# Scores of head pairs on partition halves, low half of the attended rows on GpSimd, and a reordered start, in a gated cross-attention and feed-forward kernel

## The chip, the cores and the metric

The kernel runs on one core of a Trainium2 chip. The time is device microseconds of one execution; the profile comes from one profiled execution. TensorE is called PE below, VectorE DVE, ScalarE ACT, GpSimd POOL and SyncE SP. SP mostly issues DMAs.

## What is computed

```
# x, ctx: 16 batches of 256 rows x 256 columns, fp32
x = x + tanh(g_xattn) * attention(layernorm(x), ctx, ctx)   # 16 heads of 16 dims, softmax
x = x + tanh(g_ffn) * ffn(layernorm(x))                     # 4-bit weights, 16-bit activations

attention:  q = Q @ Wq.T + bq; k = K @ Wk.T + bk; v = V @ Wv.T + bv
            scores = q @ k.T / sqrt(16); attn = softmax(scores)
            out = (attn @ v) @ Wo.T + bo
ffn:        gate, up, product and sums are rounded to 16 bits by a scale over the whole tensor
```

## The kernel before, in words

`attention` computes the first line for all 16 batches and leaves y and its LayerNorm (`lnall`); `feed_forward` computes the second. The change touches `attention` only, and the order in which the host lays out the columns of Wq, Wk and their biases.

Precision: each fp32 operand of a projection is split into a high and a low fp16 part, and three products are summed (high x high, high x low, low x high), so one projection is 12 matmuls of 256 columns (`project`, `split_product`, L418). ACT makes the high part of a result out of PSUM (`high`, `high_of`), DVE (or POOL) the low part (`low`, `low_of`).

The order of work is written out by hand as one software pipeline. All engines walk the same list of steps, `STEPS = range(-40, PAIRS * NB + 31)`. A step g is one pair of heads of one batch; a batch has 8 steps. `batch(g, off)` gives the batch whose work with offset `off` falls on step g. In steady state the work of a step depends on g mod 8 only; "step 0" to "step 7" below mean this number. On PE, each step has these parts in this order:

- the scores of batch it+1 for the maximum (L516): q and k of the pair are stacked on partitions as high, high, low of q against high, low, high of k, 96 rows. Four matmuls of 256 columns: two query tiles (tt) x two heads of the pair (r). Both heads of one tile go to one PSUM bank, `s_ps[tt]`. The two heads share the rows of `kst`; `qst` holds two copies, in which the rows of the other head are zero (the third index, r). DVE reduces each bank to the row maxima (`negm`, L880) and increments `max_done`; a bank may be written again when its own reduction is done.
- the transposed scores of batch it (L531), two matmuls of 512 columns (both heads), 97 rows: the 97th holds ones in `kst` and the negated maximum in `qst`. ACT takes the exponential (L694) into `pt`.
- in steps 5, 7, 1 and 3 the projections of v, of the output, of q and of k (the last three for other batches; L418)
- in steps 2, 4, 6 and 0 the values (L455): 16 matmuls of fp32 that write 32 partitions each
- in steps 4 and 0 the transposes of the maxima (L431), in step 6 the transposes of the normalised x (L591, `xn`).

DVE does the two reductions of the step first and then: y (step 0), its statistics (1), the low half of q (2), statistics of x (3), the low half of k and the reciprocal of the denominators (4), the low half of the attended rows `al` (5, `low_of`, L838), the maximum over `lnall` (6), the low half of x (7); in steps 5 to 7 of the first nine batches also work on the feed-forward weights. POOL does in steps of its own: `cl` (1, L1019), `at` (2), the root and LayerNorm of y (2, L988, L990, L1038), `normalise` for x (step 4, L988, L990, L999), which waits for the transposes of step 6 (`xt_done`), `xb` (6), weight pieces (7 and 0). The LayerNorm is `(x - mean) * rstd` in one instruction.

SP issues per batch: the stack of q in 6 DMAs (`stack_q`, 2 heads x 3), the stack of k in 3 (`stack_k`), the maxima in 2 x 2 (`load_tops`), and loads and stores. PE waits at step 0 for `stack_loaded`. Before step 0 of batch 0 lies a start in which weights are split, an identity matrix is built through DRAM (`ident_dram`), batch 0 is projected (q, then k, then v), and stacks are set to zero.

Of the kernel before, what the change touches and what calls it, by code (L numbers as in the profile page):

```python
# [5 lines left out]
ALU = mybir.AluOpType  # L6
# [10 lines left out]
P = 128  # L17
# [12 lines left out]
def attention(nc, t, x, ctx, out):  # L30
# [26 lines left out]
    with ExitStack() as es:  # L57
# [30 lines left out]
        ones = sb("ones", [P, 1], F32)  # L88
# [7 lines left out]
        rstd = sb("rstd", [P, KT], F32)  # L96
        xh = sb("xh", [P, 2, S], F16)
# [5 lines left out]
        kst = sb("kst", [97, 3, PAIRS, S], F16)  # L103
        qst = sb("qst", [97, 3, 2, PAIRS, S], F16)
# [18 lines left out]
        rstd2 = sb("rstd2", [P, 2, KT], F32)  # L123
        recl = sb("recl", [P, 2, 16], F32)
# [29 lines left out]
        zeros_written = sem("zeros_written")  # L154
        ones_written = sem("ones_written")
# [3 lines left out]
        qst_zeroed = [sem(f"qst_zeroed{i}") for i in range(3)]  # L159
        half_set = sem("half_set")  # L160
        w_loaded = sem("w_loaded")
# [83 lines left out]
        rstd2_done = sem("rstd2_done")  # L245
        ln_done = sem("ln_done")
        lnmax_done = sem("lnmax_done")
        lmax_done = sem("lmax_done")
        lmax_turned = sem("lmax_turned")
        ltop_done = sem("ltop_done")  # L250
        ltop_spread = sem("ltop_spread")
# [27 lines left out]
        ident_dram = nc.dram_tensor("ident_dram", (P * P,), F32, kind="Internal").ap()  # L279

# [3 lines left out]
        def _(sp):  # L284
# [11 lines left out]
            def stack_q(b):  # L296
                n = b % 3
                sp.wait_ge(qh_done, b + 1)
                if b >= 3:
                    sp.wait_ge(st_done, UNITS * (b - 2))  # L300
                sp.wait_ge(qst_zeroed[n], 1)
                for d, i in enumerate((0, 0, 1)):
                    if d == 2:
                        sp.wait_ge(ql_done, b + 1)
# [37 lines left out]

            load_x(0)
            sp.wait_ge(ident_zeroed, 2)
            sp.dma_start(ident_dram.rearrange("(p q) -> p q", p=P), ident[:]).then_inc(zeros_written, 16)
            for n in "qkv":
                sp.dma_start(wf[n], t["w" + n].rearrange("(t p) e -> p t e", p=P)).then_inc(w_loaded, 16)
            load_c(0)
            sp.wait_ge(zeros_written, 16)
            sp.dma_start(ident_dram[0:P * P:P + 1].rearrange("(p o) -> p o", o=1), ones[:],  # L350
                         allow_slow_non_contiguous=True).then_inc(ones_written, 16)
            load_x(1)
            sp.dma_start(bqk[:, 0, :], t["bq"]).then_inc(b_loaded, 16)
            sp.dma_start(bqk[:, 1, :], t["bk"]).then_inc(b_loaded, 16)
            sp.wait_ge(ones_written, 16)
            sp.dma_start(ident[:], ident_dram.rearrange("(p q) -> p q", p=P)).then_inc(ident_set, 16)
            load_c(1)
            sp.dma_start(wstage[:].rearrange("p (f d) -> p f d", d=D),
                         t["w_gate"].rearrange("(f p) d -> p f d", p=P)).then_inc(wn_loaded[0], 16)
# [4 lines left out]
            sp.dma_start(bvc[:], t["bv"]).then_inc(wo_loaded, 16)  # L364

# [48 lines left out]
        def _(pe):  # L414
# [89 lines left out]
            pe.wait_ge(ident_set, 16)  # L504
            for g in STEPS:
                it, j = divmod(g, PAIRS)
                if 0 <= it + 1 < NB:
                    b = it + 1
                    if j == 0:
                        pe.wait_ge(stack_loaded[b % 2], 144 * (b // 2 + 1))  # L510
                    for tt in range(KT):
                        u = UNITS * b + KT * j + tt
                        if u >= 2:
                            pe.wait_ge(max_done, u - 1)
                        for r in range(2):
                            mm = nc.tensor.matmul(s_ps[tt][:, r, :], qst[0:96, b % 3, r, j, tt * P:(tt + 1) * P],  # L516
                                                  kst[0:96, b % 3, j, :], start=True, stop=True)
                        mm.then_inc(s_done, 1)
                if 0 <= it < NB:
                    b = it  # L520
                    if g == 0:
                        pe.wait_ge(ones_set, 1)
                    if j == 0:
                        pe.wait_ge(top_loaded[0], 32 * (b + 1))
                    if j == QA:
                        pe.wait_ge(top_loaded[1], 32 * (b + 1))
                    for kt in range(KT):
                        u = UNITS * b + KT * j + kt
                        if u >= 3:
                            pe.wait_ge(exp_done, u - 2)  # L530
                        nc.tensor.matmul(st_ps[u % 3][:], kst[:, b % 3, j, kt * P:(kt + 1) * P],  # L531
                                         qst[:, b % 3, :, j, :], start=True, stop=True).then_inc(st_done, 1)

                if (b := batch(g, V)) is not None:
# [3 lines left out]
                    pe.wait_ge(weights_low, 3)  # L538
# [11 lines left out]
                if (b := batch(g, Q)) is not None:  # L550
                    pe.wait_ge(y_done, before(g, PROJ))
                    pe.wait_ge(v_taken, before(g, V))
                    pe.wait_ge(ql_done, b)
# [1263 lines left out]
```

## Time and profile before

| | us |
|---|---|
| median of 3 runs (600.8, 605.62, 606.33) | 605.62 |
| the profiled execution, its time | 602.64 |
| the profiled execution, its span | 600.80 |
| busy: PE / DVE / ACT / POOL | 561.2 / 490.0 / 438.6 / 206.3 |
| attention stage, first to last instruction (chain of waits enters the feed-forward) | 0 to 331.2 |
| feed-forward stage | 331.2 to 600.8 |

An instruction's time in the profile is from its start to its end; matmuls are pipelined, so that several of them overlap, and the distance of their starts says what each costs the engine. "x4" in a timeline row means that four instructions are merged, and the time is that of all of them. Idle time of an engine before an instruction stands in brackets with what ended it.

### The profile page before, as it was taken

What the parts mean: (1) busy time and instruction counts of PE and PEld (TensorE: products, weight loads), DVE (VectorE), ACT (ScalarE), POOL (GpSimd) and SP (SyncE); (2) the same over time, 40 slices, a digit from 0 to 9 for tenths busy, and PEclk for the clock granted to TensorE, in tenths of its full rate; (3) what the DMA queues carried; (4) which work ended last, traced back from release to release, by engine and by line L of the source; (5) the groups of instructions that cost most, each with busy time, mean ns of one, the idle gap of its engine ahead of it and who ended that gap; (6) DMA issues with size and microseconds to landing.
All of it is one profiled execution on the core that took longest, in us unless ns stands there. A gap on an engine that the chain in (4) does not pass through costs nothing. (4 is left out here: it accounts for less than half of the span.)

```text
span 600.8 us, 11772 instructions
## 1 busy us (share of the span) xinstructions
PE 561.2 (93%) x4337; PEld 341.6 (57%) x4337; DVE 490.0 (82%) x832; ACT 438.6 (73%) x633; POOL 206.3 (34%) x227
## 2 busy tenths in 40 slices
PE   1679999999999999999987999999999899989998
PEld 1446666666666666666446444444444344458887
DVE  5688889999999988999838699979987799964542
ACT  2227888788788877888675344549999998889960
POOL 3722358766667879765346000000000000010100
PEclk9989999999999999999999899999999999999999
DMA  6532444454554454333231000000000000023443
GB/s 184 148 89 83 134 130 128 127 145 129 152 147 140 132 139 126 96 105 109 71 102 71 3 0 1 0 1 1 1 1 0 1 0 1 0 71 106 141 141 106
DMA packets 42812, 48.98 MB, mean 82 GB/s; under 512 B 10436, under 2 KB 30532, under 8 KB 42756
## 3 DMA queue, kind: packets, MB, share of 16 engines
q1 hardware_dynamic: 40916, 43.38, 24.6%
q0 software_dynamic: 1408, 4.46, 2.6%
q8 instruction: 35, 0.57, 0.4%
q10 hardware_dynamic: 432, 0.39, 0.3%
q14 instruction: 21, 0.17, 0.1%
HBM read 24.32 MB, written 8.70 MB: 55 GB/s over the span
## 5 line engine op out<-in xcount | busy, mean ns | idle before, releaser
L880 DVE TENSOR_REDUCE negm<-s_ps 128x2 bf16<-128x512 f32 x256 | 163.1, 681 | 21.3 <-PE s_ps L516 20.1
L694 ACT ACTIVATE pt<-st_ps 128x512 f32<-128x512 f32 x256 | 138.8, 596 | 48.0 <-PE st_ps L531 46.8
L1218 PE MATMUL pairs<-xq,wut 128*128 128x512 f16 x576 | 124.7, 379 | 2.7 <-ACT lnall L1412 1.6
L1218 PEld LDWEIGHTS pairs<-xq,wut 128*128 128x128 f16 x576 | 56.2, 98 | 71.1 <-issue 2.3
L516 PE MATMUL s_ps<-kst,qst 96*128 96x256 f16 x512 | 80.7, 275 | 8.9 <-DVE negm L880 5.5
L531 PE MATMUL st_ps<-qst,kst 97*128 97x512 f16 x256 | 76.5, 380 | 1.3 <-ACT pt L694 0.8
L455 PE MATMUL pv_ps<-pt,vt 128*32 128x256 f32 x1024 | 68.5, 385 | 1.4 <-ACT ot L638 0.7
L1732 POOL PARTITION_ALL_REDUCE vmax<-vmax x5 | 1.8, 355 | 193.1 <-DVE vmax L1525 119.4
L516 PEld LDWEIGHTS s_ps<-kst,qst 96*128 96x128 f16 x512 | 44.4, 98 | 31.7 <-DVE negm L880 18.3
L1218 PE MATMUL pairs<-xq,wgt 128*128 128x512 f16 x276 | 60.5, 379 | 0.0
L999 POOL TENSOR_SCALAR xn<-xt,mv,rstd 128x256 f32<-128x256 f32 x30 | 36.5, 1223 | 55.5 <-PE misc L591 55.3
L1324 PE MATMUL pairs<-wdt,h 128*128 128x256 f16 x384 | 47.2, 273 | 2.9 <-DVE h L1687 2.3
L455 PEld LDWEIGHTS pv_ps<-pt,vt 128*32 128x32 f32 x1024 | 26.9, 109 | 38.8 <-issue 25.3
L1352 ACT COPY gb<-pairs 128x1024 f32<-128x1024 f32 x24 | 24.3, 1012 | 32.6 <-PE pairs L1218 32.6
L1218 PEld LDWEIGHTS pairs<-xq,wgt 128*128 128x128 f16 x276 | 26.8, 98 | 31.1
L1324 PEld LDWEIGHTS pairs<-wdt,h 128*128 128x128 f16 x384 | 37.3, 98 | 8.1 <-issue 2.8
L631 ACT ACTIVATE qk<-misc,bqk_s 128x256 f16<-128x256 f32 x64 | 26.9, 473 | 15.7 <-PE misc L418 15.7
L1038 POOL TENSOR_SCALAR lnall<-y,mv,rstd 128x256 f32<-128x256 f32 x28 | 34.4, 1235 | 1.5
L1594 DVE CUSTOM_DVE_ANT_0 gb<-lnall 128x1024 f32<-128x1024 int16 x24 | 29.1, 1219 | 7.0 <-ACT lnall L1384 6.8
L1587 DVE TENSOR_REDUCE cmax<-pairs 128x1 f32<-128x1024 f32 x24 | 29.3, 1222 | 1.6 <-PE pairs L1218 1.6
L1412 ACT ACTIVATE lnall<-pairs,scal 128x1024 int16<-128x1024 f32 x23 | 25.3, 1110 | 5.9 <-PE pairs L1218 5.8
L785 DVE SCALAR_TENSOR_TENSOR qk<-misc,bqk_s,qk 128x256 f16<-128x256 f32 x64 | 27.8, 476 | 2.2 <-ACT qk L631 2.2
(217 smaller groups left out, 1032.9 us busy)
## 6 DMA issues: line engine op xcount, KB each, us to landing
qst<-qk SPq DMA_DIRECT2D x96, 64.0 KB, 2.0
kst<-qk SPq DMA_DIRECT2D x45, 128.0 KB, 3.2
xt<-in_x SPq DMA_DIRECT2D x16, 256.0 KB, 4.3
ct<-in_ctx SPq DMA_DIRECT2D x16, 256.0 KB, 2.9
xr<-in_x SPq DMA_DIRECT2D x16, 256.0 KB, 4.1
out<-y SPq DMA_DIRECT2D x16, 256.0 KB, 4.0
lnall<-out POOLq DMA_DIRECT2D x8, 512.0 KB, 4.2
recb<-rec_dram SPq DMA_DIRECT2D x15, 256.0 KB
```

The source lines that it names most:

```text
L455: mm = nc.tensor.matmul(pv_ps[32 * c:32 * c + 32, u % 2, :], vt[:, b % 3, kt, 8 * (c // 2) + 2 * u + c % 2, :], pt[:, u % 2, c // 2, kt, c ...
L516: mm = nc.tensor.matmul(s_ps[tt][:, r, :], qst[0:96, b % 3, r, j, tt * P:(tt + 1) * P], kst[0:96, b % 3, j, :], start=True, stop=True)
L531: nc.tensor.matmul(st_ps[u % 3][:], kst[:, b % 3, j, kt * P:(kt + 1) * P], qst[:, b % 3, :, j, :], start=True, stop=True).then_inc(st_done, 1)
L694: nc.scalar.activation(pt[:, (j // 2) % 2, j % 2, kt], st_ps[u % 3][:], ACT.Exp, scale=1.0 / (WS * WS * HD ** 0.5)).then_inc(exp_done, 1)
L785: op = nc.vector.scalar_tensor_tensor(out=qk[:, 2 * i + 1, e, :], in0=frm[:, e, :], scalar=bqk_s[:, i, e:e + 1], in1=qk[:, 2 * i, e, :], o ...
L880: nc.vector.tensor_reduce(negm[:, b % 2, tt, lo:lo + 5:4], s_ps[tt][:], AX.X, ALU.max, negate=True).then_inc(max_done, 1)
L999: op = nc.gpsimd.tensor_scalar(xn[:, tt, :], xt[:, b % 3, tt, :], mv[:, tt, 0:1], rstd[:, tt:tt + 1], ALU.subtract, ALU.mult)
L1038: nc.gpsimd.tensor_scalar(t["lnall"][:, b, tt * D:(tt + 1) * D], y[:, b % 2, tt, :], mv2[:, b % 2, tt, 0:1], rstd2[:, b % 2, tt:tt + 1], A ...
L1218: mm = nc.tensor.matmul(ps[:, p, k, :], w[:, a, dt, f * P:(f + 1) * P], xq[:, b, c, dt, :], start=n == 0, stop=n == len(terms) - 1)
L1324: mm = nc.tensor.matmul(to, lh, wdt[:, h, f, :], start=n == 0, stop=n == len(terms) - 1)
L1587: nc.vector.tensor_reduce(cmax[:, 1, PR * c + p:PR * c + p + 1], ps[:, p], AX.XY, ALU.max, apply_absolute_value=True).then_inc(u_max, 1)
L1594: nc.vector.tensor_tensor_reduce(gb[:, c, 2 * p:2 * p + 2].rearrange("p f w -> p (f w)"), ia[:, d, 2 * p:2 * p + 2].rearrange("p f w -> p ...
```

## The change

1. Scores: `kst` and `qst` become 128 rows high. The high, high and low rows of a head dimension lie on neighbouring partitions (4k, 4k+1, 4k+2), the first head of a pair on partitions 0 to 63, the second on 64 to 127; row 63 and row 127 hold ones and the maximum. There is one copy of q. A score matmul has 63 rows, a transposed one 64; all have 256 columns, and the heads alternate. A PSUM bank of the scores now holds one head for both query tiles.
2. The stacks are 3 DMAs each for q and k, the maxima 1 instead of 2.
3. `al` moves from DVE to POOL (same step, 5, ahead of `xb`).
4. LayerNorm on POOL becomes `x * rstd + shift`, with `shift = -mean * rstd` computed by two instructions on 128x2. `normalise` moves from step 4 to step 7.
5. The start: each weight has its own semaphore; the identity is made by POOL (`affine_select`); k of batch 0 is projected ahead of q, into `st_ps[0]`; `cl` of batch 0 is made on DVE; kst and qst are zeroed whole; 12, 4 and 5 spare matmuls of 512 columns are put on PE; ACT issues the first stacks; gate work moves from steps -12 and -10 to -6 and -5.

The diff, cut to its core:

```diff
-        kst = sb("kst", [97, 3, PAIRS, S], F16)
-        qst = sb("qst", [97, 3, 2, PAIRS, S], F16)
+        kst = sb("kst", [P, 3, PAIRS, S], F16)
+        qst = sb("qst", [P, 3, PAIRS, S], F16)
...
             def stack_q(b):
                 for d, i in enumerate((0, 0, 1)):
...
-                    for r in range(2):
-                        lo = 32 * d + r
-                        sp.dma_start(qst[lo:lo + 31:2, n, r].rearrange("p j q -> p (j q)"),
-                                     qk[r:P:2, i].rearrange("p h q -> p (h q)")).then_inc(stack_loaded[b % 2], 16)
+                    sp.dma_start(qst[d:P:4, n].rearrange("p j q -> p (j q)"),
+                                 qk[:, i].rearrange("p h q -> p (h q)")).then_inc(stack_loaded[b % 2], 16)
             def stack_k(b):
...
-                    sp.dma_start(kst[32 * d:32 * d + 32, n].rearrange("p j q -> p (j q)"),
+                    sp.dma_start(kst[d:P:4, n].rearrange("p j q -> p (j q)"),
             def load_tops(b, hf):
-                for r in range(2):
-                    sp.dma_start(qst[96:97, b % 3, r, QA * hf:QA * hf + QA, :], mrow[QA * r:QA * r + QA, hf, :]
-                                 ).then_inc(top_loaded[hf], 16)
+                sp.dma_start(qst[63:P:64, b % 3, QA * hf:QA * hf + QA, :], mrow[:, hf, :]).then_inc(top_loaded[hf], 16)
...
+            def spare_products(n):
+                for _ in range(n):
+                    nc.tensor.matmul(s_ps[0][:].rearrange("p a b -> p (a b)"), kst[0:63, 1, 0, 0:P],
+                                     kst[0:63, 1, 0:2].rearrange("p j q -> p (j q)"), start=True, stop=True)
+            pe.wait_ge(kst_zeroed, 1)
+            spare_products(12)
+            pe.wait_ge(weights_low, 1)
+            pe.wait_ge(cl_done, 1)
+            project(st_ps[0], "k", ch, cl, k_done)
+            spare_products(4)
+            pe.wait_ge(ident_set, 1)
...
                     for tt in range(KT):
-                        u = UNITS * b + KT * j + tt
-                        if u >= 2:
-                            pe.wait_ge(max_done, u - 1)
                         for r in range(2):
-                            mm = nc.tensor.matmul(s_ps[tt][:, r, :], qst[0:96, b % 3, r, j, tt * P:(tt + 1) * P],
-                                                  kst[0:96, b % 3, j, :], start=True, stop=True)
-                        mm.then_inc(s_done, 1)
+                            u = UNITS * b + 2 * j + r
+                            if tt == 0 and u >= 2:
+                                pe.wait_ge(max_done, u - 1)
+                            mm = nc.tensor.matmul(s_ps[r][:, tt, :], qst[64 * r:64 * r + 63, b % 3, j, tt * P:(tt + 1) * P],
+                                                  kst[64 * r:64 * r + 63, b % 3, j, :], start=True, stop=True)
+                            if tt == KT - 1:
+                                mm.then_inc(s_done, 1)
...
                     for kt in range(KT):
-                        u = UNITS * b + KT * j + kt
-                        if u >= 3:
-                            pe.wait_ge(exp_done, u - 2)
-                        nc.tensor.matmul(st_ps[u % 3][:], kst[:, b % 3, j, kt * P:(kt + 1) * P],
-                                         qst[:, b % 3, :, j, :], start=True, stop=True).then_inc(st_done, 1)
+                        for r in range(2):
+                            u = UNITS * b + 2 * j + r
+                            if kt == 0 and u >= 3:
+                                pe.wait_ge(exp_done, u - 2)
+                            mm = nc.tensor.matmul(st_ps[u % 3][:, kt, :],
+                                                  kst[64 * r:64 * r + 64, b % 3, j, kt * P:(kt + 1) * P],
+                                                  qst[64 * r:64 * r + 64, b % 3, j, :], start=True, stop=True)
+                            if kt == KT - 1:
+                                mm.then_inc(st_done, 1)
...
+                    if b == 0:
+                        spare_products(5)
+                        pe.wait_ge(weights_low, 2)
                     pe.wait_ge(xl_done, b + 1)
                     project(bank(g), "q", xh, xl, q_done)
-                if (b := batch(g, K)) is not None:
+                if (b := batch(g, K)) is not None and b:
...
-                if (b := batch(g, 21)) is not None and b < LAST - 1:
-                    low_of(b)
...
+                nc.gpsimd.tensor_scalar(negative, r, -1.0, 0.0, ALU.mult, ALU.add).then_inc(done, 1)
+                pool.wait_ge(done, 2 * b + 1)
+                nc.gpsimd.tensor_tensor(to, mean, negative, ALU.mult).then_inc(done, 1)
+                pool.wait_ge(done, 2 * b + 2)
...
-                        op = nc.gpsimd.tensor_scalar(xn[:, tt, :], xt[:, b % 3, tt, :], mv[:, tt, 0:1],
-                                                     rstd[:, tt:tt + 1], ALU.subtract, ALU.mult)
+                        op = nc.gpsimd.tensor_scalar(xn[:, tt, :], xt[:, b % 3, tt, :], rstd[:, tt:tt + 1],
+                                                     shift[:, tt:tt + 1], ALU.mult, ALU.add)
...
+            nc.gpsimd.affine_select(out=ident[:], in_=ident[:], compare_op=ALU.not_equal, fill=1.0, base=0,
+                                    pattern=[[-1, P]], channel_multiplier=1).then_inc(ident_set, 1)
...
+            nc.gpsimd.memset(qst[:].rearrange("p n j q -> p (n j q)").bitcast(I32), 0).then_inc(qst_zeroed, 1)
...
+                if (b := batch(g, 21)) is not None and b < LAST - 1:
+                    pool.wait_ge(ah_done, b + 1)
+                    pool.wait_ge(o_done, b)
+                    nc.gpsimd.tensor_tensor(al[:], at[:, b % 2], ah[:], ALU.subtract).then_inc(al_done, 1)
...
-                if (b := batch(g, -28)) is not None and b:
+                if (b := batch(g, -25)) is not None and b >= 2 or g == PAIRS - 28 and (b := 1):
                     normalise(b)
```

## Rows read from the trace of the kernel before

**Rows 1.** Table of windows: length, busy time and instructions of each engine, clock, DMA.
```profile
core 0: us, PE busy (x) PEld busy (x) DVE busy (x) ACT busy (x) POOL busy (x), PEclk, DMA share, GB/s
43.00:285.69 242.69, 239.93 (x2309) 157.28 (x2309) 222.93 (x459) 196.62 (x406) 157.01 (x167) 1.00 0.44 125
111.02:128.33 17.31, 17.31 (x170) 11.52 (x168) 16.23 (x36) 13.64 (x28) 12.49 (x14) 1.00 0.46 134
```

**Rows 2.** Timeline of PE, one batch: start, length, engine, line, operation, count.
```profile
111.02 0.60 PE L516 MATMUL s_ps<-kst,qst 96*128 96x256 f16 x4
...
113.08 0.61 PE L516 MATMUL s_ps<-kst,qst 96*128 96x256 f16 x4
...
115.28 0.60 PE L516 MATMUL s_ps<-kst,qst 96*128 96x256 f16 x4
...
117.24 0.61 PE L516 MATMUL s_ps<-kst,qst 96*128 96x256 f16 x4
...
123.69 0.60 PE L516 MATMUL s_ps<-kst,qst 96*128 96x256 f16 x4
...
126.15 0.60 PE L516 MATMUL s_ps<-kst,qst 96*128 96x256 f16 x4
```

**Rows 3.** Timeline of PE from one step's transposed scores to the next step's.
```profile
102.56 0.60 PE L531 MATMUL st_ps<-qst,kst 97*128 97x512 f16 x2
103.09 1.07 PE L455 MATMUL pv_ps<-pt,vt 128*32 128x256 f32 x16
103.98 0.27 PE L431 MATMUL misc<-identb,negm 128*8 128x128 bf16 x2
104.19 0.61 PE L516 MATMUL s_ps<-kst,qst 96*128 96x256 f16 x4
104.63 0.60 PE L531 MATMUL st_ps<-qst,kst 97*128 97x512 f16 x2
105.07 0.38 PE L418 MATMUL misc<-wh_v,ch 128*128 128x256 f16 x2
```

**Rows 4.** Timeline of DVE, reductions of the same batch.
```profile
113.62 1.28 DVE L880 TENSOR_REDUCE negm<-s_ps 128x2 bf16<-128x512 f32 x2
...
115.76 1.26 DVE L880 TENSOR_REDUCE negm<-s_ps 128x2 bf16<-128x512 f32 x2
...
117.72 1.28 DVE L880 TENSOR_REDUCE negm<-s_ps 128x2 bf16<-128x512 f32 x2
...
119.92 1.26 DVE L880 TENSOR_REDUCE negm<-s_ps 128x2 bf16<-128x512 f32 x2
...
122.14 1.22 DVE L880 TENSOR_REDUCE negm<-s_ps 128x2 bf16<-128x512 f32 x2
...
124.23 1.23 DVE L880 TENSOR_REDUCE negm<-s_ps 128x2 bf16<-128x512 f32 x2
...
126.57 1.29 DVE L880 TENSOR_REDUCE negm<-s_ps 128x2 bf16<-128x512 f32 x2 [0.42 <-PE s_ps L516]
```

**Rows 5.** Groups of instructions by line: count, busy us, mean ns, idle before.
```profile
L1038 POOL TENSOR_SCALAR lnall<-y,mv,rstd 128x256 f32<-128x256 f32 x28 | 34.4, 1235 | 1.5
...
L990 POOL TENSOR_TENSOR rstd<-ve,half 128x2 f32<-128x2 f32 x32 | 22.9, 717 | 2.7
...
L1019 POOL TENSOR_TENSOR cl<-ct,ch 128x512 f16<-128x512 f32 x15 | 17.3, 1154 | 8.5 <-ACT ch L720 8.5
...
L838 DVE TENSOR_TENSOR al<-at,ah 128x512 f16<-128x512 f32 x15 | 12.0, 802 | 3.7 <-ACT ah L661 3.7
...
L988 POOL TENSOR_SCALAR ve<-mv 128x2 f32<-128x2 f32 x32 | 6.2, 195 | 32.3 <-DVE mv L758 21.1 <-issue 7.6 <-DVE mv L806 1.4
```

**Rows 6.** Timeline of all engines, the start up to the first scores.
```profile
10.59 1.11 PE L591 MATMUL misc<-ident,xn 128*128 128x128 f32 x4 [10.59 <-DMA ident<-ident_dram]
...
17.01 0.88 DVE L785 SCALAR_TENSOR_TENSOR qk<-misc,bqk_s,qk 128x256 f16<-128x256 f32 x2 [2.21 <-ACT qk L631]
...
19.97 1.99 ACTq L707 DMA_DIRECT2D kst<-qk  x3
...
25.78 0.61 PE L516 MATMUL s_ps<-kst,qst 96*128 96x256 f16 x4 [2.58 <-DMA kst<-qk]
```

More of the change, by code:

```diff
@@ L158, in attention @@
         ones_set = sem("ones_set")
-        qst_zeroed = [sem(f"qst_zeroed{i}") for i in range(3)]
+        kst_zeroed = sem("kst_zeroed")
+        qst_zeroed = sem("qst_zeroed")
         half_set = sem("half_set")
-        w_loaded = sem("w_loaded")
+        wk_loaded = sem("wk_loaded")
+        wq_loaded = sem("wq_loaded")
+        wv_loaded = sem("wv_loaded")
         b_loaded = sem("b_loaded")
@@ L341, in spread_rec, with load_w @@
                              ).then_inc(rec_loaded, 16)
+            def load_w(n, done):
+                sp.dma_start(wf[n], t["w" + n].rearrange("(t p) e -> p t e", p=P)).then_inc(done, 16)
             load_x(0)
[L344 to L352, printed above, removed]
+            load_w("k", wk_loaded)
             sp.dma_start(bqk[:, 0, :], t["bq"]).then_inc(b_loaded, 16)
             sp.dma_start(bqk[:, 1, :], t["bk"]).then_inc(b_loaded, 16)
[L355 to L359, printed above, removed]
+            load_c(0)
+            load_w("q", wq_loaded)
+            load_w("v", wv_loaded)
+            load_x(1)
             sp.dma_start(gx[:], t["gx"].rearrange("(o d) -> o d", o=1).broadcast_to((P, 1))).then_inc(g_loaded, 16)
@@ L676, in _ @@
                     if b:
-                        act.wait_ge(stack_loaded[(b - 1) % 2], 144 * ((b - 1) // 2 + 1))
-                    act.wait_ge(bias_scaled, 1)
+                        act.wait_ge(stack_loaded[(b - 1) % 2], 96 * ((b - 1) // 2 + 1))
                     high(0, bank(PAIRS * b + Q), qh_done)
-                if (b := batch(g, -12)) is not None:
+                    if b == 0:
+                        act.wait_ge(qst_zeroed, 1)
+                        act.wait_ge(ql_done, 1)
+                        act.dma_start(qst[2:P:4, 0].rearrange("p j q -> p (j q)"),
+                                      qk[:, 1].rearrange("p h q -> p (h q)")).then_inc(stack_loaded[0], 16)
+                if (b := batch(g, -12)) is not None and b:
                     act.wait_ge(k_done, b + 1)
@@ L690, in _ @@
                         act.wait_ge(pv_done, 4 * b + j // 2 - 1)
-                    for kt in range(KT):
-                        u = UNITS * b + KT * j + kt
+                    for r in range(2):
+                        u = UNITS * b + 2 * j + r
                         act.wait_ge(st_done, u + 1)
-                        nc.scalar.activation(pt[:, (j // 2) % 2, j % 2, kt], st_ps[u % 3][:], ACT.Exp,
+                        nc.scalar.activation(pt[:, (j // 2) % 2, j % 2, :, r], st_ps[u % 3][:], ACT.Exp,
                                              scale=1.0 / (WS * WS * HD ** 0.5)).then_inc(exp_done, 1)
@@ L857, in _, with weight_low @@
             nc.vector.memset(ident[:], 0.0).then_inc(ident_zeroed, 1)
-            nc.vector.memset(ones[:], 1.0).then_inc(ident_zeroed, 1)
             nc.vector.memset(half[:], -0.5).then_inc(half_set, 1)
             nc.vector.memset(row1[:], 1.0).then_inc(half_set, 1)
+            nc.vector.memset(kst[:].rearrange("p n j q -> p (n j q)").bitcast(I32), 0).then_inc(kst_zeroed, 1)
+            nc.vector.memset(ones16[:].bitcast(I32), ONES).then_inc(kst_zeroed, 1)
             normal_stats(0)
-            nc.vector.memset(qst[:, 1].rearrange("p r j q -> p (r j q)").bitcast(I32), 0).then_inc(qst_zeroed[1], 1)
+            def weight_low(n, m):
+                dve.wait_ge(weights_high, m)
+                nc.vector.scalar_tensor_tensor(out=wl[n][:], in0=wf[n][:], scalar=WS, in1=wh[n][:],
+                                               op0=ALU.mult, op1=ALU.subtract).then_inc(weights_low, 1)
+            weight_low("k", 1)
+            dve.wait_ge(ch_done, 1)
+            nc.vector.tensor_tensor(cl[:], ct[:, 0], ch[:], ALU.subtract).then_inc(cl_done, 1)
+            dve.wait_ge(b_loaded, 32)
+            nc.vector.tensor_scalar(bqk_s[:], bqk[:], WS, None, ALU.mult).then_inc(bias_scaled, 1)
+            weight_low("q", 2)
             dve.wait_ge(rstd_done, 1)
@@ L867, in _ @@
             op.then_inc(xn_ready, 1)
-            for n, m in zip("qkv", range(3)):
-                dve.wait_ge(weights_high, m + 1)
-                nc.vector.scalar_tensor_tensor(out=wl[n][:], in0=wf[n][:], scalar=WS, in1=wh[n][:],
-                                               op0=ALU.mult, op1=ALU.subtract).then_inc(weights_low, 1)
+            dve.wait_ge(kh_done, 1)
+            dve.wait_ge(bias_scaled, 1)
+            low(1, st_ps[0], kl_done)
             for g in STEPS:
@@ L891, in _ @@
                     normal_stats(b)
-                if (b := batch(g, -12)) is not None:
+                if (b := batch(g, -12)) is not None and b:
                     dve.wait_ge(kh_done, b + 1)
```

116 lines of the change are left out of this document (64 added, 52 removed).

## The prediction

> **What bounds the kernel now.** I read the table of windows first, then the timeline of one batch on TensorE and on VectorE. The program has two stages. The feed-forward from 331 us on is not touched by the diff. The attention stage is. In its steady part, the 14 batches from 43.00 to 285.69 us, PE is busy 239.93 of 242.69 us, DVE 222.93, ACT 196.62 and POOL 157.01; one batch of eight steps takes 17.31 us, with PE busy for all of it and DVE for 16.23 [rows 1]. The starts of the score matmuls say that it is an issue limit and not a chain of waits: step 0 takes 113.08 - 111.02 = 2.06 us, step 1 2.20, step 2 1.96, step 6 126.15 - 123.69 = 2.46 [rows 2]. Steps 3, 5 and 7 are like step 1 and step 4 is like step 0, which adds up: 2 x 2.06 + 4 x 2.19 + 1.96 + 2.46 = 17.3. So PE is the bound, and DVE is only 1.08 us per batch behind it. What is saved on PE pays until DVE takes over.
>
> **The scores on PE.** Per step, the four 256-column score matmuls (96 rows) take 104.63 - 104.19 = 0.44 us, and the two 512-column ones for the exponentials (97 rows) take 105.07 - 104.63 = 0.44 [rows 3]: 0.11 us for 256 columns in both. After the change the two heads of a pair lie on partitions 0-62 (63) and 64-126 (127), in turn, into different banks. If the two halves of the array work side by side, each group needs two rounds of 0.11 instead of four: 0.22 + 0.22 saved, 0.44 us per step. The trace of before has no matmul on row halves. Bounds: nothing saved (they run in turn, as all matmuls on the full array do here), or 0.44. The nearest row for the good end is the value product: its 16 matmuls, on four column groups, take only 103.98 - 103.09 = 0.89 us [rows 3], a quarter of 16 single 0.22 us slots (3.5). I take 0.44, since these run side by side already.
> The Trainium skill ("TensorE: Matmul & The Clock Gate", part 3 on packing small matmuls) says the same of row groups; no run so far shows it for them.
>
> **What the halves cost.** Two 512-column matmuls from 102.56 would be through at 102.56 + 0.44 = 103.00; the value products begin at 103.09. After them two 128-column matmuls from 103.98 are through at 104.09, and the scores begin at 104.19 [rows 3]. So going into and out of the column groups costs 0.1 us each. Now the scores are a shape of their own too. Steps 1, 3, 5 and 7 (scores, then a full-array projection) get two more changes of shape, step 6 one more (its transposes on the full array stand ahead of the next scores), steps 0, 2 and 4 none, because their neighbours are value products or the 8-column turns of the maxima, which follow the value products without a gap. Nine changes at 0.1 us are 0.9 us per batch. Bounds: 0, and 0.25 each (2.2).
> The Trainium skill ("TensorEngine Tiling (Array Packing)", key properties under tiling modes) has the rule that speaks against the change: a change of tiling mode drains TensorE. The page gives no price. Two 256-column matmuls take 0.38 us of which 0.22 is their turn on the array [rows 3], so a full emptying would be 0.16 us: 1.4 us per batch instead of 0.9. The rows show 0.1, and the sum goes by them; what the rule says happens is what they show.
> New step times of PE alone: steps 0 and 4 2.06 - 0.44 = 1.62; step 2 1.52; odd steps 2.20 - 0.44 + 0.2 = 1.96; step 6 2.46 - 0.44 + 0.1 = 2.12. Sum 14.7 us per batch.
>
> **DVE takes over.** Where DVE had no wait, the distance from one pair of reductions to the next is DVE's own step: 115.76 - 113.62 = 2.14 in step 1, 1.96 in step 2, 2.20 in step 3, 2.22 in step 4, 2.09 in step 5, 126.57 - 124.23 - 0.42 idle = 1.92 in step 6 [rows 4]. The change takes the low half (0.80 us in the mean of 15 [rows 5]) out of step 5.
> There is also a new lock step. Now each bank holds one head for both query tiles, and the matmuls alternate between the banks, so the first pair already needs both reductions of the step before; until now the first bank was refilled under the second reduction. From the scores' start to the reduction is 126.57 - 126.15 = 0.42 us [rows 2, 4]; the pair of reductions takes 1.28; for the semaphore I take 0.08, as the gap of 0.09 above. So no step is shorter than 0.42 + 1.28 + 0.08 = 1.78 us. A step's other DVE work (y, statistics, low halves of q and k, transposed x) lies in that gap and hides it where it is 0.6 us or more. Only step 5, emptied of its low half, shows it, and there PE's 1.96 is longer.
> Taking the longer of the two engines in each step: 1.8, 2.14, 1.96, 2.20, 2.22, 1.96, 2.12, 1.96 = 16.4 us. I add 0.1 for the steps in which the preparation of the feed-forward weights lies (DVE work of steps 5 and 6 in the first nine batches): 16.5. Fourteen batches: 242.7 - 231.0 = 11.7 us saved. Bounds per batch: DVE's bare 16.23 - 0.80 = 15.4, and 17.5 if the other DVE work comes too late to fill half of the gaps.
>
> **POOL.** It gets the low half; the same operation for the context takes 1.15 us on POOL [rows 5]. The LayerNorm as multiply-add needs two more operations on 128x2 each time, twice a batch: four, between 0.20 (the small scalar operation) and 0.72 each (the power), so 0.8 to 2.9 us; I take 1.1, as a plain multiply is nearer to the first. The large operation itself was 1.23 us; as multiply and add it lies between 0.6 (half of the 512 elements of the 1.15 us row) and 1.25; I take 1.2, for the sum does not hang on it. POOL then has 12.49 + 1.15 + 1.1 = 14.7 us in a batch of 16.5. Its waits for the transposes (normalise sits one stage ahead of them now, and is moved from step 4 to step 7, behind them) go. What hangs on it, `al` before the output projection of step 7, and `lnall` before the maximum of step 6, is then about a step early. So nothing is charged. If that cover is gone (upper end, 16.5 us of work), PE waits for `al`: some 0.5 us per batch.
> SP issues three q stacks instead of six and one row of maxima instead of two, so the queue that also carries the k stack is emptier. The steps being shorter takes 0.7 us from the k stack's way between its low half and its first use, and the three issues saved give that back. I charge nothing.
>
> **The start.** Now the identity goes through DRAM, transposes start at 10.59, the low half of q is done at 17.01 + 0.88, k's comes after it and its stack is issued at 19.97; scores start at 25.78, 5.81 later [rows 6]. After: POOL makes the identity, the transposes also need its reciprocal root, so I leave them near 10.6. K's projection is ahead of x's, on a PE kept busy by spare products. Left is q's path: low half at 17.9, or 16 if the projection runs at full speed (four transposes of 1.11 us show that PE is slow there [rows 6]); then one DMA on ACT's queue instead of three, about 3.6 us to the first score. That is 19.6 to 21.5; I take 19.7, since the spare products are many: 6.1 us saved. Bounds: 3 (the zeroing of all of qst on POOL, and the second x, become the last), and 8. The batch behind it, 43.00 - 25.78 = 17.2, I put at 16.7: 0.5 saved. The tail after 285.69 has no score reductions for most of its length and hangs on ACT and DMA: 0.5 saved.
>
> **Sum.** 6.1 + 0.5 + 11.7 + 0.5 = 18.8 us. The profiled execution took 602.64 us (span 600.80 and 1.84 around it): 583.8. The median shown is 605.62, 3 us above it, with runs from 600.8 on: against it 586.8. I forecast 585.5, between them.
>
> **Rivals.**
> 1. The halves don't overlap (the change doesn't do what it says). Then PE keeps its 17.31 and gets the nine changes of shape: 18.2 us per batch, 14 x 0.9 = 12.6 slower, about 1 more in the two ends, less 6.1 at the start: 602.6 + 7.5 = 610. It decides if the second matmul of a pair starts about 0.11 us behind the first; break-even is 17.7 us a batch. For it: nothing on row halves in the trace; against: the column groups overlap. Chance 0.08.
> 2. The lock step costs in most steps: 17.3 to 17.5 us per batch, and only the start gains: 602.6 - 6.6 + 1 = 597. For it: DVE within 8% of PE before, and DVE work that itself waits for ACT in the same step (the low halves). Against: before, that work came without a wait. Chance 0.17.
> 3. DVE is never left waiting, 15.6 us a batch, POOL's traffic on it lower: 14 x 0.9 less, 573. For: DVE had slack only of its own making; against: PE is longer in steps 5 to 7. Chance 0.10.
> The forecast, 576 to 593, has 0.65.
>
> **Chances and range.** A measurement of this kernel tells about 1% from no change. Faster by over 1% means under 599.6: the forecast, rival 3 and most of rival 2 (0.12 of its 0.17): 0.87. Within 1%: 0.05, the upper end of rival 2. Slower: 0.08, rival 1. The range leaves out rival 1 and the ends of the others: 575 to 600.
>
> **What would show it.** Right: pairs of score matmuls within some 10 ns of each other; a batch of 16.2 to 16.8 us; DVE busy over 94% of it, with idle left before the reductions of steps 5 to 7; gaps of 0.1 us at the projections; first score near 20 us; `al` on POOL near 1.15. Wrong: pairs 0.11 us apart (rival 1); waits of the reductions for the scores in steps 1 to 4 (rival 2); PE waiting for `al` or for the k stack; first score after 23 us.

## The result and the profile after

The changed kernel takes 589.0 us (588.25 to 589.84, 4 runs), the one before 604.47 beside it (600.8 to 606.33, 4 runs): a ratio of 0.9745, interval 0.9714 to 0.9777. The profiled execution went from 602.64 to 588.25 us, 14.4 less.

The windows of the changed kernel, cut at the first score (21.47), the end of the first pass (40.90), the end of the steady part (271.89) and the start of the feed-forward (near 316.8); inside them the first batch of the steady part and one later batch. Columns: length, busy us (instructions) of PE, PE weight loads, DVE, ACT, POOL, then the granted clock as a share of full, DMA share, GB/s.

```profile
0.00:21.47 21.47, 14.71 (x66) 7.11 (x67) 12.30 (x32) 7.75 (x15) 9.16 (x18) 1.00 0.67 208
21.47:40.90 19.43, 14.30 (x79) 7.33 (x79) 15.10 (x31) 3.86 (x9) 5.40 (x12) 0.73 0.29 91
40.90:58.60 17.70, 16.33 (x157) 9.07 (x157) 14.08 (x30) 12.12 (x26) 3.45 (x7) 0.82 0.24 80
40.90:271.89 230.99, 219.71 (x2533) 133.26 (x2534) 218.44 (x447) 193.19 (x406) 148.38 (x224) 0.99 0.43 132
107.47:123.66 16.19, 15.63 (x185) 9.60 (x185) 15.68 (x35) 13.42 (x28) 12.13 (x19) 1.00 0.49 142
```

Beside [rows 1]: the 14 steady batches went from 242.69 to 230.99 us, 11.7 less, just what was forecast. The start gave 25.78 - 21.47 = 4.3 (forecast 6.1), the first pass took 19.43 instead of 17.22 (2.2 lost, 0.5 gained was forecast), the tail to the feed-forward gave 0.6 (forecast 0.5). That is 14.4 for a forecast of 18.8. Both misses lie before 40.90. The exact hit on the steady part has luck in it: its first batch took 17.70 us at a granted clock of 0.82 (15.80 at full clock, in `warm` below), a loss that the forecast didn't have, and the later ones made up for it.

One batch on PE, the rows that answer to [rows 2, 3]: start, us from first start to last end, then the operation.

```profile
107.47 0.39 PE L529 MATMUL s_ps<-kst,qst 63*128 63x256 f16 x4
...
109.11 0.53 PE L529 MATMUL s_ps<-kst,qst 63*128 63x256 f16 x4
...
111.00 0.38 PE L419 MATMUL misc<-xh,wl_q 128*128 128x256 f16 x2
111.32 0.39 PE L529 MATMUL s_ps<-kst,qst 63*128 63x256 f16 x4
111.54 0.38 PE L546 MATMUL st_ps<-qst,kst 64*128 64x256 f16 x4
111.86 1.07 PE L456 MATMUL pv_ps<-pt,vt 128*32 128x256 f32 x16
112.86 0.74 PE L529 MATMUL s_ps<-kst,qst 63*128 63x256 f16 x4
...
115.17 0.41 PE L529 MATMUL s_ps<-kst,qst 63*128 63x256 f16 x4
...
116.83 0.28 PE L529 MATMUL s_ps<-kst,qst 63*128 63x256 f16 x1
117.38 0.39 PE L529 MATMUL s_ps<-kst,qst 63*128 63x256 f16 x3 [0.27 <-DVE negm L924]
...
118.15 0.39 PE L419 MATMUL misc<-wh_v,ch 128*128 128x256 f16 x2 [0.17 <-DVE qk L818]
...
119.57 0.39 PE L529 MATMUL s_ps<-kst,qst 63*128 63x256 f16 x4
```

Four score matmuls of 256 columns now have their turn in 111.54 - 111.32 = 0.22 us, where four took 0.44 before: the halves of the array work side by side. After the last pair (0.22 from 111.00) the next shape would start at 111.22 and starts at 111.32; after the scores at 111.76 the value products start at 111.86. A change of shape is 0.10 us here too.

The same stretch on DVE, which answers to [rows 4]:

```profile
107.90 1.29 DVE L924 TENSOR_REDUCE negm<-s_ps 128x2 bf16<-128x512 f32 x2
...
109.76 1.28 DVE L924 TENSOR_REDUCE negm<-s_ps 128x2 bf16<-128x512 f32 x2
...
111.90 1.26 DVE L924 TENSOR_REDUCE negm<-s_ps 128x2 bf16<-128x512 f32 x2
...
113.85 1.28 DVE L924 TENSOR_REDUCE negm<-s_ps 128x2 bf16<-128x512 f32 x2
...
116.06 1.26 DVE L924 TENSOR_REDUCE negm<-s_ps 128x2 bf16<-128x512 f32 x2
117.23 0.87 DVE L818 SCALAR_TENSOR_TENSOR qk<-misc,bqk_s,qk 128x256 f16<-128x256 f32 x2
...
118.27 1.23 DVE L924 TENSOR_REDUCE negm<-s_ps 128x2 bf16<-128x512 f32 x2
...
120.00 1.30 DVE L924 TENSOR_REDUCE negm<-s_ps 128x2 bf16<-128x512 f32 x2
...
122.13 1.30 DVE L924 TENSOR_REDUCE negm<-s_ps 128x2 bf16<-128x512 f32 x2 [0.15 <-PE s_ps L529]
```

DVE has hardly a gap: 15.68 of 16.19 us, against PE's 15.63 (before: PE 17.31 of 17.31). Neither is full; they wait for each other for some 0.5 us each.

POOL's lines, with the mean ns of one, which answer to [rows 5]; each of the two new small operations on 128x2 takes 0.19 us:

```profile
L1081 POOL TENSOR_TENSOR al<-at,ah 128x512 f16<-128x512 f32 x14 | 16.2, 1157 | 29.7 <-ACT ah L682 29.7
L1089 POOL TENSOR_SCALAR lnall<-y,rstd,shift 128x256 f32<-128x256 f32 x28 | 15.3, 555 | 1.5
```

The start on PE, against [rows 6], and after it the row of q's low half on DVE:

```profile
4.39 5.30 PE L508 MATMUL s_ps<-kst 63*128 63x512 f16 x12 [4.39 <-DVE kst L893]
9.62 0.61 PE L419 MATMUL st_ps<-ch,wh_k 128*128 128x256 f16 x2
...
13.70 0.66 PE L612 MATMUL misc<-ident,xn 128*128 128x128 f32 x4
...
15.84 0.38 PE L419 MATMUL misc<-xh,wh_q 128*128 128x256 f16 x2 [0.31 <-DVE xl L975]
...
21.47 0.39 PE L529 MATMUL s_ps<-kst,qst 63*128 63x256 f16 x4 [0.44 <-DMA qst<-qk]
...
33.58 0.32 PE L529 MATMUL s_ps<-kst,qst 63*128 63x256 f16 x1 [2.38 <-DVE negm L924]
```

```profile
18.22 0.88 DVE L818 SCALAR_TENSOR_TENSOR qk<-misc,bqk_s,qk 128x256 f16<-128x256 f32 x2 [0.45 <-ACT qk L652]
```

The transposes stand at 13.70 instead of 10.59: twelve spare products hold PE until 9.69, k's projection runs at half speed (0.43 us per two from 9.62 on; the 1.00 in the table's first window doesn't show it, the starts do), four spares follow it, and only then come the transposes. From 13.70 on the way to the end of q's low half takes 5.4 us (18.22 + 0.88 = 19.10), as forecast (10.6 to 16), with q's projection at full speed (0.22 per two).

### The profile page after: what moved, and what is told of

It reads as the page before. It is cut to its first block and busy times, and to the rows that moved or that the text cites. A ratio compares the mean times of both kernels' runs of the same rounds, so it can differ in the third digit from the quotient of the medians.

```text
span 586.4 us, 12288 instructions
## 1 busy us (share of the span) xinstructions
PE 544.4 (93%) x4614; PEld 317.1 (54%) x4614; DVE 483.0 (82%) x818; ACT 435.1 (74%) x633; POOL 191.8 (33%) x298
## 5 line engine op out<-in xcount | busy, mean ns | idle before, releaser
L529 PE MATMUL s_ps<-kst,qst 63*128 63x256 f16 x512 | 66.9, 282 | 16.6 <-DVE negm L924 13.7
L546 PE MATMUL st_ps<-qst,kst 64*128 64x256 f16 x512 | 56.4, 272 | 1.7 <-ACT pt L732 1.7
L529 PEld LDWEIGHTS s_ps<-kst,qst 63*128 63x128 f16 x512 | 20.6, 94 | 54.7 <-DVE negm L924 39.7
L546 PEld LDWEIGHTS st_ps<-qst,kst 64*128 64x128 f16 x512 | 30.7, 96 | 6.8 <-ACT pt L732 3.7
L1688 DVE TENSOR_TENSOR gb<-lnall 128x1024 f32<-128x1024 int16 x23 | 27.2, 1216 | 2.5 <-ACT lnall L1468 2.4
L1700 DVE TENSOR_REDUCE cmax<-gb 128x1 f32<-128x2048 f32 (+2 forms) x16 | 27.8, 1746 | 0.0
```

The source lines that it names most:

```text
L529: mm = nc.tensor.matmul(s_ps[r][:, tt, :], qst[64 * r:64 * r + 63, b % 3, j, tt * P:(tt + 1) * P], kst[64 * r:64 * r + 63, b % 3, j, :], s ...
L546: mm = nc.tensor.matmul(st_ps[u % 3][:, kt, :], kst[64 * r:64 * r + 64, b % 3, j, kt * P:(kt + 1) * P], qst[64 * r:64 * r + 64, b % 3, j, ...
L1688: nc.vector.tensor_tensor(gb[:, c, 2 * p:2 * p + 2], ia[:, c % 2, 2 * p:2 * p + 2], ib[:, c % 2, 2 * p:2 * p + 2], ALU.mult).then_inc(p3_d ...
L1700: nc.vector.tensor_reduce(cmax[:, 3, n:n + 1], flat[:, first:last], AX.X, ALU.max, apply_absolute_value=True).then_inc(p3_max, 1)
```

## The experiments

Twelve kernels, in four groups; each group had its own runs of the kernel before beside it (medians 604.21, 603.53, 604.73 and 604.55 us). Ratios are to those, with 95% intervals. The first four went together, then `after_control` to `warm`, then `before_al_norm` to `warm_stats5`, then the last.

**same_half: both heads of a pair on one half.** Edit, the same at all four places of the scores (the second head's scores are then made from the first head's rows):

```diff
-qst[64 * r:64 * r + 63, b % 3, j, tt * P:(tt + 1) * P]
+qst[0:63, b % 3, j, tt * P:(tt + 1) * P]
```

> The changed kernel, but both heads of a pair use partitions 0 to 63 for the scores (the second head is computed from the first head's rows, so that half of the attention is of the wrong head; the number and sizes of the matmuls stay). If the gain comes from the two halves working side by side, the four score matmuls of a step take 0.44 us again instead of 0.22, both kinds, the batch goes from 16.2 to about 18.2 us (14.7 + 8 x 0.44 on TensorE), and the time to about 589 + 14 x 2 + 2 = 619 us, slower than the kernel before. If the gain came from the low half on GpSimd or from the start, the time stays within 3 us of 589.

619.87 us (2 runs), ratio 1.0246 (1.0177 to 1.0315). Window of one batch, and its first matmuls:

```profile
119.76:138.02 18.26, 18.26 (x186) 12.19 (x185) 16.00 (x35) 13.88 (x28) 11.77 (x19) 1.00 0.40 125
```

```profile
119.76 0.61 PE L529 MATMUL s_ps<-kst,qst 63*128 63x256 f16 x4
120.20 0.60 PE L546 MATMUL st_ps<-qst,kst 64*128 64x256 f16 x4
```

0.44 us for four again, PE busy for all of 18.26 us: 17.31 and the nine changes of shape. This is rival 1 made on purpose; its batch of 18.2 was right. With all the rest of the change in place, the one edit is worth 2.07 us a batch and 31 us in all.

**al_dve: the low half of the attended rows back on DVE, in step 5.**

```diff
-                    nc.gpsimd.tensor_tensor(al[:], at[:, b % 2], ah[:], ALU.subtract).then_inc(al_done, 1)
...
+                if (b := batch(g, 21)) is not None and b < LAST - 1:
+                    low_of(b)
```

> The changed kernel with the low half of the attended rows back on VectorE, in step 5. Theory: in step 5 TensorE is the longer one (its v projection waits for the low half of k), so the 0.7 us fit into VectorE's slack: 0 to 0.3 us per batch, 589 to 592 us. Rival: VectorE sets the batch and every us on it counts: 0.7 per batch, 599 us.

587.21 us, ratio 0.9718 (0.9679 to 0.9758); the changed kernel has 0.9745 (0.9714 to 0.9777).

```profile
107.12:123.31 16.19, 15.63 (x186) 9.60 (x186) 16.05 (x36) 13.43 (x28) 10.45 (x18) 1.00 0.44 140
```

The same 16.19 us, with DVE at 16.05 instead of 15.68. The move to POOL brings nothing: from step 5's reductions to step 6's DVE now takes 2.10 us instead of 1.73, and from there to step 7's 1.82 instead of 2.13. PE sets the pace there, and DVE has room.

**ln_old: the LayerNorms as before (subtract, then multiply), without the two small operations.**

```diff
-                                                     shift[:, tt:tt + 1], ALU.mult, ALU.add)
+                                                     rstd[:, tt:tt + 1], ALU.subtract, ALU.mult)
```

> The changed kernel with the LayerNorm on GpSimd in its old form (subtract, multiply; no shift). GpSimd gets 4 x 0.67 us more and 4 x 0.2 us less per batch, 1.9 us, 14.0 of 16.2 busy. Theory: its results are due a step later or more, so 588 to 591 us. Rival: GpSimd is on the path through the low half and the output projection, 1 us per batch or more, 603 us and up.

587.46 us, ratio 0.9721 (0.9678 to 0.9763), the batch 16.19 us. POOL has slack either way; nothing hangs on the form.

**r_outer: the score matmuls for the maxima ordered by head, then by tile**, so the first bank is filled before the second is needed.

```diff
-                    for tt in range(KT):
-                        for r in range(2):
+                    for r in range(2):
+                        for tt in range(KT):
```

> The changed kernel with the score matmuls for the maximum ordered by head first, tile second: a bank is filled again as soon as its own reduction is done, but two neighbours are on the same half. Theory: TensorE loses 0.1 us per step where it is the longer one, and gains 0.3 us where it waits for the second reduction now (steps 1, 3 to 5): 586 to 591 us. Rival (the lock step of both reductions is what keeps the batch at 16.2): 0.6 us per batch gained, 581 us.

586.77 us, ratio 0.9706 (0.9668 to 0.9744), the batch 16.19 us.

```profile
110.49 0.40 PE L529 MATMUL s_ps<-kst,qst 63*128 63x256 f16 x4
110.72 0.39 PE L546 MATMUL st_ps<-qst,kst 64*128 64x256 f16 x4
```

The four still pass in 0.23 us. I read it so that the second tile of the first head runs beside the first tile of the second head; that reading is argued, the 0.23 is measured. That starts need not keep the program's order shows elsewhere in this batch: a transposed score matmul starts at 108.51, the last of the four before it at 108.54. What follows is that the order of the four decides nothing here, and that a lock step between the banks costs nothing that this edit could give back.

**after_control: the changed kernel again**, beside those that follow.

> The changed kernel once more, on the same chip as the three beside it: 587 to 589 us, and again a long stretch at the lower clock after the first scores if that belongs to the kernel and not to the one execution.

589.43 us (587.59 to 592.53), ratio 0.9767 (0.9742 to 0.9793).

**before_al_pool: the kernel before, with only the low half moved to POOL.**

```diff
-                    low_of(b)
...
+                    nc.gpsimd.tensor_tensor(al[:], at[:, b % 2], ah[:], ALU.subtract).then_inc(al_done, 1)
```

> The kernel before with only the low half of the attended rows moved from VectorE to GpSimd. TensorE is busy for the whole batch there, so theory: no change, ratio 0.997 to 1.003. Rival: VectorE's 16.2 of 17.3 us holds TensorE up in places, 0.2 us per batch or more gained, ratio 0.995 or less.

649.23 us (645.77 to 652.07), ratio 1.074 (1.0715 to 1.0765): a miss by 45 us. A batch takes 20.58 us. POOL and PE in step 7 of one:

```profile
140.51 2.43 POOL L997 TENSOR_SCALAR xn<-xt,mv,rstd 128x256 f32<-128x256 f32 x2 [5.44 <-PE misc L591]
142.91 1.15 POOL L1033 TENSOR_TENSOR al<-at,ah 128x512 f16<-128x512 f32 x1
```

```profile
139.67 0.66 PE L591 MATMUL misc<-ident,xn 128*128 128x128 f32 x4
...
144.32 0.60 PE L418 MATMUL misc<-wo,ah 128*128 128x256 f16 x4 [3.12 <-POOL al L1033]
```

Read it backwards: PE waits 3.12 us for `al`; `al` stands in POOL's order behind the normalise, which waited 5.44 us for the transposes of step 6 to free its buffer. Behind the instruction that waits, a ready one waits as well.

**gate_back: the gate work (its products and DVE's part) back from steps -6 and -5 to -12 and -10**, against the loss in the first pass.

```diff
-                if g == -6:
+                if g == -12:
```

> The changed kernel with the gate work put back from steps -6 and -5 to -12 and -10 (VectorE 1.5 us of it, TensorE four fp32 matmuls). Theory: the 2.4 us in which TensorE waits for VectorE at step -4 shrinks by 1.5, the first pass goes from 19.4 to 18 us, and if the lower clock after it comes from that gap, another 2 us: 584 to 586 us. Rival: the work then delays the first scores by as much, 587 to 589.

590.96 us, ratio 0.9786 (0.9763 to 0.9809), not better than the control: a miss. The first pass was shorter in its profile (18.44), but the first score later (23.65) and the batch behind at 18.12, at a granted clock of 0.81. PE's wait of 2.38 us was 0.99 here, as meant, and the lower clock stayed. The gate work by itself isn't the cause.

**warm: 21 spare products of 512 columns at the ends of steps -9 to -1**, into a bank that is free there.

```diff
+                if g in {-9: 4, -8: 4, -7: 1, -6: 1, -5: 4, -4: 2, -3: 1, -2: 2, -1: 2}:
+                    warm_products(...)
```

> The changed kernel with 21 more spare matmuls on TensorE in steps -9 to -1, where it is idle between the scores. Theory: the first pass and the batch after it lose 4 us to the lower clock (0.73 of full in the first pass); kept at full clock the first pass takes 17 us instead of 19.4 and batch 1 16.2 instead of 17.7: 584 to 585 us. Rival: the spare matmuls themselves delay the scores by what the clock gives: 587 to 590.

585.03 us (584.41 to 586.57), ratio 0.9695 (0.9673 to 0.9716): 4.4 below the control on the same chip. The first pass and the first steady batch:

```profile
21.71:39.81 18.10, 15.44 (x96) 7.76 (x96) 14.95 (x31) 3.59 (x8) 5.07 (x12) 0.91 0.28 92
39.81:55.61 15.80, 13.81 (x156) 8.12 (x157) 14.09 (x30) 12.08 (x26) 3.45 (x7) 1.00 0.28 90
```

The granted clock goes from 0.73 to 0.91 and from 0.82 to 1.00; 37.13 us together become 33.90, by PE doing more.

**before_al_norm: before_al_pool, with the normalise also moved to step 7**, as the change does.

```diff
-                if (b := batch(g, -28)) is not None and b:
+                if (b := batch(g, -25)) is not None and b >= 2 or g == PAIRS - 28 and (b := 1):
                     normalise(b)
```

> The kernel before with the low half on GpSimd and normalise moved behind the transposes it waits for (step 7 instead of 4), as in the change. The low half alone cost 45 us. Theory: it sat on GpSimd's queue behind normalise, which waits for the transposes of step 6, and the output projection of step 7 waits for it; with normalise behind it the cost goes: ratio 0.995 to 1.005 to the kernel before. Rival: GpSimd is simply too slow for it in any order (a batch of 18 us or more): ratio 1.04 or more.

603.48 us (12 runs), ratio 0.9976 (0.9959 to 0.9993).

```profile
129.10:146.41 17.31, 17.31 (x171) 11.51 (x169) 16.67 (x34) 14.08 (x29) 13.62 (x15) 1.00 0.63 176
```

The 45 us are gone and PE is busy for the whole 17.31 us again: the move of the normalise is what makes `al` on POOL free, and without the halves the two together bring 0.2% (0.1 to 0.4).

**stats5: the statistics of x (DVE, 0.84 us) from step 3, where DVE is late, to step 5**, which lost its low half.

```diff
-                if (b := batch(g, -29)) is not None and b >= 3:
+                if (b := batch(g, -27)) is not None and b >= 3:
                     normal_stats(b)
```

> The changed kernel with the statistics of x moved on VectorE from step 3 to step 5, where the low half has left room. Theory: steps 1 to 4 are set by VectorE and steps 5 to 7 by TensorE, and the v projection of step 5 waits for the low half of k, so VectorE is 1 us earlier there: a batch of 15.5 us instead of 16.2 in 11 batches, 580 to 583 us. Rival: VectorE's total sets the batch wherever the work stands: 587 to 590 us.

588.63 us, ratio 0.9725 (0.9699 to 0.9752), no gain over the changed kernel; a batch near 16.1 instead of 15.5: a miss. DVE around what was step 3:

```profile
114.80 1.28 DVE L924 TENSOR_REDUCE negm<-s_ps 128x2 bf16<-128x512 f32 x2
116.54 1.30 DVE L924 TENSOR_REDUCE negm<-s_ps 128x2 bf16<-128x512 f32 x2 [0.47 <-PE s_ps L529]
```

On DVE step 3 went from 2.21 to 1.74 us (116.54 - 114.80), with 0.47 of it idle, and step 5 from 1.73 to 2.49: step 5 hadn't the room, and moving work within the batch moved the wait.

**warm_stats5: both edits together.** 

> Both improvements on the changed kernel: statistics of x in step 5 and the spare matmuls in the first pass, which gave 4.4 us by themselves. If they add up: 576 to 579 us.

584.41 us (584.05 to 584.93, 4 runs), ratio 0.9655 (0.9629 to 0.9682): the lowest median of the study, and a miss by 5 us and more. The intervals of it and of warm alone overlap, so the gain shown is warm's.

**warm_stats5_cut: the same with fewer spares ahead of the transposes.**

```diff
-            spare_products(12)
+            spare_products(7)
...
-            spare_products(4)
```

> The last version with fewer spare matmuls ahead of the first transposes: 7 instead of 12 before k's projection and none behind it. In the changed kernel they hold k's projection back by about 1.9 us (its operands are there at 7.7, it starts at 9.62) and the transposes until 13.70, where the kernel before had them at 10.59. Theory: transposes at about 11.3, first scores 1.5 to 2 us earlier than with all of them (21.05 in that run), 582 to 583.5 us. Rival: without them the clock rises later, q's projection runs at half of it, and the first scores stay at 21: 584 to 586 us.

585.84 us (582.46 to 586.89, 6 runs), ratio 0.9695 (0.9675 to 0.9714). PE in its profiled execution, which was the fastest of the six:

```profile
7.64 0.59 PE L419 MATMUL st_ps<-ch,wh_k 128*128 128x256 f16 x2
...
10.86 0.63 PE L617 MATMUL misc<-ident,xn 128*128 128x128 f32 x4 [0.50 <-DVE xn L917]
...
19.77 0.39 PE L534 MATMUL s_ps<-kst,qst 63*128 63x256 f16 x4
```

In that execution the transposes stand near the forecast's 10.6, q's projection still runs at full speed and the first score starts at 19.77 (forecast 19.7). The median doesn't follow: it lies above the forecast of 582 to 583.5 and isn't below that of warm_stats5. The other five runs have no trace, so what they lost is open.

## Why the prediction was right, and where it was off

**PE is the bound, the halves overlap (right).** The forecast of 0.44 us a step and nine changes of shape at 0.1 us is what same_half measured from the other side: without the overlap 18.26 us, PE always busy. The Trainium skill ("TensorE: Matmul & The Clock Gate", part 3) says that row groups run together; the trace now agrees, 0.22 us against 0.44. By the Trainium skill ("TensorEngine Tiling (Array Packing)", key properties) a change of tiling mode drains the engine. The trace has 0.10 us at such a change, as the column groups had it in [rows 3], less than the 0.16 that the prediction put for a full emptying.

**DVE takes over, 16.5 us a batch (right, step by step too, when read on DVE).** Measured: 230.99 / 14 = 16.5, a later batch 16.19. From one pair of reductions to the next (the rows above) it is 1.86, 2.14, 1.95, 2.21, 2.21, 1.73, 2.13 and, for step 7, the 1.96 that is left of 16.19, for a forecast of 1.8, 2.14, 1.96, 2.20, 2.22, 1.96, 2.12, 1.96. Only step 5 is clearly off. PE's own starts give another split: 1.64, 2.21, 1.54, 2.31, 1.66, 2.74, 2.13 and 1.96 us. They mislead, because the first matmul of a step needs only the first bank's reduction and starts early, and the others wait (112.86, whose four take 0.74 instead of 0.39).

Two parts of the reasoning were not as written. "No step is shorter than 1.78 us": the shortest is 1.54 on PE and 1.73 on DVE. And step 5 was put at PE's 1.96. On PE it took 2.74, with two waits: for the reductions of step 4 (0.27 in the row), and with the v projection for the low half of k (0.17), which DVE can only do behind them. That wait was not charged. On DVE the same step took 1.73, 0.23 less than forecast. From the v projection on PE is the slower one up to the next batch. al_dve agrees (more work for DVE in step 5, no more time), and so does stats5 (0.47 us gained in step 3, 0.76 lost in step 5).

**POOL (no charge: right, with sizes off).** `al` took 1.16 us (forecast 1.15). The large operation as multiply and add took 0.555 us, not 1.2: it lay below the lower bound of 0.6 given. The two small ones are 0.19 each, 0.78 for four (forecast 1.1). POOL's batch is 12.13 us, not 14.7. ln_old shows that the form of the LayerNorm doesn't reach the time. That POOL's waits for the transposes go was the weightiest line of that part, though it carried no number: on the kernel before, `al` on POOL without it costs 45 us. No run undoes it on the changed kernel. The forecast had priced the lost cover at 0.5 us a batch, and before_al_pool shows 20.58 - 17.31 = 3.3. My own expectation for that run missed it, since it asked only what DVE's time is worth, and not what POOL's order would do.

**The start (4.3 for 6.1).** The step that failed is "so I leave them near 10.6". The spares and k's projection stand ahead of the transposes on PE, whatever POOL and DVE have ready. That made 3.1 us. Of q's two ways, the fast one was right (full speed), and from the end of the low half to the score it took 21.47 - 19.10 = 2.4 us for 3.6, which gave 1.2 back. warm_stats5_cut shows 10.86 and 19.77 when the spares are fewer.

**The first pass (2.2 lost for 0.5 gained).** The step that failed is the 16.7 us put for it: it had no term for PE's clock. PE has gaps there (14.30 busy of 19.43 us), and the granted clock was at its lower level, 1.2 GHz, from 23.5 to 26.9 and again, after a wait of 2.38 us that ended at 33.58, from 33.7 to 47.3, into the first steady batch. Windows of the changed kernel and of the one before (all stretches in this part in which they had the lower level):

```profile
23.50:26.90 3.40, 3.27 (x17) 1.84 (x19) 1.37 (x3) 0.00 (x0) 1.23 (x2) 0.50 0.00 0
33.70:47.30 13.60, 12.18 (x64) 6.02 (x65) 9.15 (x16) 4.42 (x9) 2.25 (x3) 0.50 0.15 49
```

```profile
27.30:30.70 3.40, 3.19 (x16) 2.26 (x16) 1.49 (x3) 0.00 (x0) 0.51 (x1) 0.50 0.00 0
37.50:41.00 3.50, 3.50 (x19) 2.62 (x18) 2.19 (x5) 0.60 (x1) 0.00 (x0) 0.51 0.65 180
```

That is 17.0 us at half clock, and 6.9 before. The first stretch is alike in both; the second is 13.6 us long instead of 3.5. after_control has 17.0 us too, in three stretches. warm has 3.4 us (33.5 to 36.9) and gets 4.4 us back by filling PE. What made it longer than before is open. It is not the wait alone: gate_back has 0.99 us of wait there and 17.1 us at half clock. Nor are the shorter scores shown to be the reason: same_half has them at their old length and 23.8 us at half clock.

**The rivals.** Rival 1 fell by the 0.22 us. Rival 2 (a lock step of 17.3 us a batch) fell by 16.5. Rival 3 (DVE never waiting) would be 15.6; DVE waits about 0.5 us a batch, so part of it is true of the best batches (15.43 the last). Of the change's parts, the halves bring the steady gain; the low half on POOL and the form of the LayerNorm bring nothing that these runs could tell from zero. The start brought 4.3 us in the trace, and the first pass took 2.2 of that back; no run has the old start with the new scores, and none takes the fewer stack DMAs by themselves.

## What to carry to other kernels

When a change makes one engine faster, put the next engine's own time beside it step by step, take the longer in each step, and check the split on the engine that is the slower one there. The total of an engine is not enough: al_dve put 0.37 us more a batch on DVE, stats5 moved work within the same total, and the batch stayed near 16.2 both times. Before moving an instruction to another engine's queue, look at what that queue's head waits for at that place, not at how busy it is: here the same 1.15 us cost 45 us or nothing. Where TensorE has gaps in a start-up, look at its granted clock: spare products in the gaps gave 4.4 us here. Spares ahead of the first real products held the transposes back by 2.8 us (13.70 against 10.86), but taking some of them out didn't lower the median.

## What the runs showed that was not expected

- POOL's operation on 128x256 f32 with two per-partition scalars takes 555 ns as multiply and add and 1221 ns as subtract and multiply (ln_old, the same place): the kind of the operation counts, not its size alone.
- DVE's clip of the feed-forward weights (128x512) slowed down where `al` ran on POOL: the six of `wstage` take 0.42 us in the mean in the kernel before and in al_dve, 1.00 here, and 0.94 in before_al_norm, which has the old scores. The line of the six, and a place where two of the three clips of `wfall` meet POOL:

```profile
L1013 DVE TENSOR_SCALAR wstage<-wi 128x512 f32<-128x512 int16 x6 | 5.9, 1004 | 0.0
```

```profile
151.68 1.27 POOL L1099 TENSOR_TENSOR xb<-xr,tbo 128x512 f32<-128x512 f32 x1
151.80 1.77 DVE L1013 TENSOR_SCALAR wfall<-wi 128x512 f32<-128x512 int16 x2
```

  Of the nine clips, the four that meet no two-input operation of POOL on 128x512 take 0.42 to 0.46 us, and the other five, which meet `xb` (now behind `al` and so later), 0.83 to 2.45. Each of the five ends about 0.28 us after `xb` does: the first of the two above takes 1.43, up to 153.23, and `xb` ends at 152.95. In the kernel before and in al_dve no clip meets one. The five cost DVE 5.1 us in all. That isn't why the move to POOL brings nothing to the batch of 16.19 us above, though: no clip lies in it.
- The two matmuls of a pair on the two halves start 3 to 4 ns apart in the changed kernel (the four at 111.32 and the four at 111.54).
